# One block from the similarity sums to the rounded adjacency, rows searched in pairs, parts added by TensorE

## The reference

```python
def _ada_gcn(xn, weight, bias):                    # xn: N=512 nodes, B=64, L=128; weight is adj
    x_norm = xn / jnp.maximum(jnp.linalg.norm(xn, axis=-1, keepdims=True), 1e-12)
    mean_sim = jnp.einsum('nbl,mbl->nm', x_norm, x_norm) / B
    k = max(int(N * 0.3), 1)                       # 153
    _, idx = jax.lax.top_k(mean_sim, k + 1)
    ...
    A = jnp.where(mask, mean_sim, 0)               # the k largest of each row, without itself
    deg = A.sum(axis=0)
    dinv = jnp.where(deg > 0, jax.lax.rsqrt(deg), 0)
    An = dinv[:, None] * A * dinv[None, :]
    xw = jnp.einsum('nbl,lo->nbo', xn, weight)
    out = jnp.einsum('sd,sbl->dbl', An, xw) + bias
    return out
...
x = _layernorm(x + _L0_gnn_ref(x, adj, L0_gnn_bias), axis=-1)       # _ada_gcn
x = _layernorm(x + _L1_gnn_ref(x, adj, ...), axis=-1)               # two kernels over 128 nodes, W matrices
x = _layernorm(x + _L2_gnn_ref(x, adj, L2_gnn_bias), axis=-1)       # _ada_gcn
x = _layernorm(x + _L3_gnn_ref(x, adj, adj, L3_gnn_bias), axis=-1)
```

## Time and profile before

| | |
|---|---|
| median of 3 runs | 1784.02 us (1780.71 to 1786.39) |
| the profiled execution | 1781.9 us, of which the span is 1779.8 us |
| busy share PE, DVE, ACT, POOL | 88%, 72%, 47%, 31% |
| mean granted clock of PE | 0.931 of full speed |
| DMA | 106.14 MB, 59 GB/s over the span |

### The profile page before, as it was taken

One profiled execution on the slowest core, in us unless ns is written; L12 is line 12 of the kernel. 1 busy time (PEld: TensorE's weight loads), 2 busy tenths in 40 slices (PEclk: granted clock), 3 DMA queues, 4 the chain that ended last, 5 costly groups with the idle time before them and its releaser, 6 DMA issues. The chain is left out here.

```text
span 1779.8 us, 27351 instructions
## 1 busy us (share of the span) xinstructions
PE 1557.4 (88%) x7776; PEld 1268.6 (71%) x7776; DVE 1286.9 (72%) x3046; ACT 828.6 (47%) x1381; POOL 548.3 (31%) x749
## 2 busy tenths in 40 slices
PE   7899470599999999999999999998599791799997
PEld 4678330478888888888888888876488691577775
DVE  5798799347766677666776667765477699599997
ACT  7775220134344443444434444343333591377775
POOL 5652020012123221232212322122100000599997
PEclk9999685799999999999999999999699895799998
DMA  5320200101001110011100111000442000244442
GB/s 210 106 72 1 94 0 0 47 25 42 24 30 47 47 41 23 30 47 47 41 22 31 47 47 41 18 12 25 171 143 95 0 0 0 71 144 146 145 143 106
DMA packets 57580, 106.14 MB, mean 60 GB/s; under 512 B 5888, under 2 KB 6016, under 8 KB 57536
## 3 DMA queue, kind: packets, MB, share of 16 engines
q1 hardware_dynamic: 57536, 105.60, 17.7%
HBM read 71.90 MB, written 33.69 MB: 59 GB/s over the span
## 5 line engine op out<-in xcount | busy, mean ns | idle before, releaser
L773 POOL TENSOR_TENSOR rs_a<-ve_a,neghalf 128x1 f32<-128x1 f32 x64 | 34.6, 541 | 495.4 <-DVE nm_a L767 495.4
L232 PE MATMUL acc<-xn_lo,xn_hi 128*128 128x512 f32 (+1 forms) x640 | 145.4, 358 | 5.0 <-DVE xn_lo L203 4.8
L198 ACT ACTIVATE xn_hi<-xn 128x512 fp32r<-128x512 f32 x128 | 80.6, 630 | 117.1 <-DVE xn L191 117.0
L232 PEld LDWEIGHTS acc<-xn_lo,xn_hi 128*128 128x128 f32 x640 | 102.3, 192 | 19.2 <-DVE xn_lo L203 10.4
L1566 PE MATMUL l_ps<-an_hi,xw_hi 128*128 128x512 f32 x256 | 105.5, 412 | 9.8 <-POOL xw_lo L1627 8.4
L223 PEld LDWEIGHTS acc<-xn_hi 128*128 128x128 f32 x512 | 95.6, 192 | 24.3 <-ACT xn_hi L198 7.7
L923 PE MATMUL l_ps<-an_hi,xw_hi 128*128 128x512 f32 x256 | 103.2, 403 | 6.5 <-DVE xw_lo L1263 6.3
L564 DVE MATCH_REPLACE8 work<-best,work 128x520 f32<-128x520 f32 x160 | 107.7, 685 | 0.0
L329 POOL TENSOR_TENSOR sq_lo<-sq,sq_hi 128x512 fp32r<-128x512 f32 x64 | 87.3, 1380 | 61.2 <-ACT sq_hi L296 61.0
L203 DVE TENSOR_TENSOR xn_lo<-xn,xn_hi 128x512 fp32r<-128x512 f32 x128 | 105.8, 827 | 0.4 <-ACT xn_hi L198 0.2
L923 PE MATMUL l_ps<-an_hi,xw_lo 128*128 128x512 f32 x256 | 101.3, 396 | 0.0
(11 more groups left out here) (239 smaller groups left out, 4869.5 us busy)
## 6 DMA issues: line engine op xcount, KB each, us to landing
xr<-in_x SPq DMA_DIRECT2D x32, 512.0 KB, 3.5
xin<-in_x SPq DMA_DIRECT2D x64, 256.0 KB, 2.6
between<-xo SPq DMA_DIRECT2D x64, 256.0 KB, 2.0
xres<-between SPq DMA_DIRECT2D x32, 512.0 KB, 3.7
xin<-between SPq DMA_DIRECT2D x64, 256.0 KB, 2.7
out<-xo SPq DMA_DIRECT2D x64, 256.0 KB, 2.0
raw_lang<-in_L_gnn_W_lang SPq DMA_DIRECT2D x1, 1024.0 KB, 5.5
raw_grav<-in_L_gnn_W_grav SPq DMA_DIRECT2D x1, 1024.0 KB, 7.9
```

The lines of the kernel that those rows point to most:

```text
L198: self.nc.scalar.activation(self.hi[:, i % 4, :], self.xn[:, i % 4, :], ACT.Copy).then_inc(self.hi_ready, 1)
L232: mm = self.nc.tensor.matmul(out, h[:, c * P:(c + 1) * P], l[:, a:b], start=False, stop=False, skip_group_check=True)
```

## The change

The three functions `whole_similarity`, `choose` and `normal_adjacency` become one function `adjacency` with one block; the two barriers between them are gone, and semaphores take their place. In particular:

- `hl` is copied to SBUF by ACT (rows 0 and 1) and DVE (rows 3 and 2) without the factor 1/64, which is now applied at the degrees.
- Row 0 of the similarity is put together as before (transposes into a bank, two additions on DVE). For the rows 1, 3 and 2 PE adds the transposed blocks of `hl_sb` and `hl_sb` itself right into the banks of `hh`, with products with the identity; ACT copies the finished rows to SBUF. The blocks under the diagonal are transposed into three different banks.
- The search takes two rows at a time: all 20 rounds of the rows 0 and 1, then all of the rows 2 and 3. It begins when rows 0 and 1 stand in `work`. Marked entries are kept (now in `sim` itself) after each pair. The masks of rows 2 and 3 come between the pairs.
- PE sums the degrees of rows 0 and 1 between the pairs. ACT takes the square root and DVE the reciprocal, in place of GpSimd's power; ACT computes a root of a small tile beforehand.
- GpSimd takes the remainders of the rows 0 and 1, DVE those of 2 and 3.
- All eight PSUM banks are held through similarity and adjacency; `an_hi` and `an_lo` and the tiles for the weights are allocated before the similarity. The weights' loads are issued at the start of the block.

```diff
+            def largest(p):
+                pair = (2 * p, 2 * p + 1)
+                dve.sem_inc(marked[p], 2)
+                with dve.Fori(0, rounds) as r:
+                    for k, c in enumerate(pair):
+                        dve.wait_ge(marked[p], 2 * r + k + 1)
+                        own_step(dve, passed)
+                        nc.vector.max(best[:, c, :], work[:, c, :]).then_inc(found[p], 1)
+                    for k, c in enumerate(pair):
+                        dve.wait_ge(found[p], 2 * r + k + 1)
+                        own_step(dve, passed)
+                        mark(p, c)
...
+                dve.wait_ge(lower, CH - 1)
+                for k, c in enumerate(pair):
+                    dve.wait_ge(marked[p], 2 * (rounds + (1 if rest else 0)) + k + 1)
+                    nc.vector.scalar_tensor_tensor(out=sim[:, c, :], in0=row_of(c), scalar=CHOSEN, in1=sim[:, c, :],
+                                                   op0=ALU.is_equal, op1=ALU.mult).then_inc(chosen, 1)
+
+            nc.vector.tensor_copy(hl_sb[:, 3, :], at.hl[3]).then_inc(dve_hl, 1)
+            nc.vector.tensor_copy(hl_sb[:, 2, :], at.hl[2]).then_inc(dve_hl, 1)
+            nc.vector.memset(work[:, :, 0:8], NEVER)
+            dve.wait_ge(act_hl, 1)
+            nc.vector.tensor_tensor(part, at.hh[0], hl_sb[:, 0, :], ALU.add).then_inc(parted, 1)
+            dve.wait_ge(t0_made, 1)
+            dve.wait_ge(parted, 1)
+            nc.vector.tensor_tensor(sim[:, 0, :], g[:], part, ALU.add).then_inc(row0, 1)
...
+            dve.wait_ge(copied, 1)
+            mask(1)
+            dve.wait_ge(masked, 2)
+            largest(0)
+            dve.wait_ge(copied, 3)
+            mask(2)
+            mask(3)
+            dve.wait_ge(masked, 4)
+            largest(1)
+
+            dve.wait_ge(summed, 1)
+            nc.vector.tensor_scalar(deg[:], g[:, 0:CH], 1.0 / nb, 1e-37, ALU.mult, ALU.max).then_inc(dve_done, 1)
+            nc.vector.tensor_scalar(pos[:], g[:, 0:CH], 0.0, None, ALU.is_gt).then_inc(dve_done, 1)
+            dve.wait_ge(rooted, 1)
+            nc.vector.reciprocal(root[:], root[:]).then_inc(dve_done, 1)
...
+            for c in (2, 3):
+                dve.wait_ge(hi_ready, c + 1)
+                nc.vector.tensor_tensor(s.an_lo[:, c, :], row_of(c), s.an_hi[:, c, :].bitcast(F32), ALU.subtract)
...
+            def add_turned(out, c, j):
+                nc.tensor.matmul(out, hl_sb[:, j, c * P:(c + 1) * P], s.ident[:], start=False, stop=False,
+                                 skip_group_check=True)
+
+            def add_plain(out, row):
+                return nc.tensor.matmul(out, s.ident[:], row, start=False, stop=True, skip_group_check=True)
...
+            for j in range(1, CH):
+                add_turned(at.hh[1][:, (j - 1) * P:j * P], 1, j)
+            add_plain(at.hh[1][:, 0:P], hl_sb[:, 1, P:2 * P])
+            add_turned(at.hh[3], 3, 3)
+            add_plain(at.hh[3], hl_sb[:, 3, 3 * P:N]).then_inc(raised, 1)
+            for j in range(2, CH):
+                add_turned(at.hh[2][:, (j - 2) * P:(j - 1) * P], 2, j)
+            add_plain(at.hh[2], hl_sb[:, 2, 2 * P:N]).then_inc(raised, 1)
+            for c in range(1, CH):
+                pe.wait_ge(row0, 1)
+                if c > 1:
+                    pe.wait_ge(upper, c - 1)
+                for j in range(c):
+                    mm = nc.tensor.transpose(turned[c][0][:, j * P:(j + 1) * P], sim[:, j, c * P:(c + 1) * P], s.ident[:])
+                mm.then_inc(low_made, 1)
...
+            act.wait_ge(raised, 1)
+            copy(sim[:, 1, P:N], at.hh[1]).then_inc(upper, 1)
+            act.wait_ge(low_made, 1)
+            copy(sim[:, 1, 0:P], h[:, 0:P]).then_inc(lower, 1)
+            act.wait_ge(lower, 1)
+            act.wait_ge(upper, 1)
+            copy(row_of(1), sim[:, 1, :]).then_inc(copied, 1)
...
+            act.wait_ge(warmed, 1)
+            nc.scalar.activation(warm[:], warm[:], ACT.Sqrt)
+            act.wait_ge(dve_done, 2)
+            nc.scalar.activation(root[:], deg[:], ACT.Sqrt).then_inc(rooted, 1)
```

More of the change, by code:

```diff
@@ L754, in first @@
+            for c in (0, 1):
+                pool.wait_ge(hi_ready, c + 1)
+                nc.gpsimd.tensor_tensor(s.an_lo[:, c, :], row_of(c), s.an_hi[:, c, :].bitcast(F32), ALU.subtract)
 def first(g):
```

404 lines of the change are left out of this document (176 added, 228 removed).

## The result

The changed kernel takes 1764.88 us (median of 4 runs, 1761.68 to 1768.1) against 1783.01 (4 runs, 1780.71 to 1786.39): ratio 0.9897, 95% interval 0.9872 to 0.9922. In a second series it was 1763.89 against 1784.28, ratio 0.9876 (0.9855 to 0.9897). The forecast was 1768, range 1760 to 1777. The profiled execution took 1764.64 us, its span is 1762.8.

The account below looks back on a forecast made before the run. DVE's serial chain, with the PE-DVE-ACT chain around it, was taken to bound both adjacencies. Terms 10.0 + 3.8 + 2.3 - 0.15 = 16.0 us off; from the runs' median of 1784.0, forecast 1768 us, range 1760 to 1777.

Parts of the forecast that it names:

- Ahead of the search: From the similarity's products to the first MAX8: 5.3 and 4.65 us off in the two adjacencies, 10.0 together.
- the unit of PE's products: One 128x128 fp32 product ahead of the search, two instructions: 0.265 us at full clock, 0.52 at half; ten units.
- The moment of the fall that I assumed: PE's clock halves ahead of the search, 2.9 and 2.2 us after ACT's first copy in the two adjacencies.
- The two PSUM copies: DVE's two copies of 512 columns out of PSUM, ahead of the search: 1.3 us for both.
- Search, choice and sums: From first MAX8 to summed degrees: 108.6 us instead of 110.48, 1.9 off in each adjacency, 3.8 in all.
- 0.76 for a block end: Price of a block end in DVE's chain at the search: 0.76 us, one of them gone.
- Behind the sums: From summed degrees to last difference: 0.65 + 0.5, 1.15 us off in each adjacency, 2.3 in all.
- the split of the differences: Behind the sums, GpSimd and DVE each take two differences: 0.5 us off in each adjacency.
- The table: The exponential's table is loaded again in the second turn of the pair of layers: 0.15 us lost.
- The loop of two rows: Rival: search turns with two rows stall; small gap, 1772 to 1783 us, chance 0.12; slower than before, 0.07.
- Time given back behind: Rival: stages behind the adjacency give the gain back, leaving under 5 us; no chance of its own, within 0.12.
- layers that change by more than 2 us: Sign that the prediction is wrong: the layers' stretch, whose code is unchanged, changes its length by over 2 us.

Follow-up runs that it names:

- e2: The changed kernel with its four rows searched in one loop again instead of in pairs; 1774.79 us, ratio 0.994.
- e3: The changed kernel with its two inner block ends back, before and after the search; pairs and PE's additions kept; 1776.82 us, ratio 0.9951.
- e8: The changed kernel with nine products of constants on PE between the similarity's last product and the first transpose; 1763.78 us.
- e11: The changed kernel with the row order of e7, five products of constants in the head, and the added products of e9 and e10; 1755.40 us, ratio 0.9842.
- e12: e11 with eleven instead of five products behind the last round, three instead of five behind the sums, eight instead of ten at the next stage's start; 1755.23 us.
- e10: e9 with further products of constants: 5 between sums and row of degrees, 22 behind it, 10 at the next stage's start; 1762.51 us, ratio 0.988.
- e7: The changed kernel with PE's transposes of row 1's lower block moved ahead of row 2's additions; 1765.08 us, ratio 0.9885.
- e9: The changed kernel with five products of constants on PE behind each of the second pair's last five rounds, before the sums; 1760.19 us.

## Why the prediction was right, point by point

- *Ahead of the search*: 10.0 us forecast, 14.2 in the first profile, 12.7 with the clock fallen in both (8.55 and 8.61). The term that was mis-sized is the unit of PE's products, at both clocks: I took 0.265 and 0.52 us, the length of a group of four units divided by four, which counts the tail of the group's last instruction in every unit. From start to start a unit is 0.42 us at half clock (1388.77, 1389.19), and from the first addition to row 1's turned block it is 3.85 us in the second head, not 5.1; at full clock it is 2.22 in the first head (191.14 to 193.36), where ten units of 0.265 make 2.65. A further 0.3 us came off behind PE. The moment of the fall that I assumed is no property of the place: the clock fell or stayed in the first heads of executions of one program. (Of the eight additions on DVE that, by the section on the change, have left it, two are still there, L562 and L565; six have gone.) The two PSUM copies (1.3) and the start of PE (1.35 forecast, 1.46) were right.
- *Search, choice and sums*: 3.8 forecast, 3.8 measured, and the steps between (51.1 us for pair 0, row 2 chosen at 104.3) stand where they were put. e2 and e3 show that pairs and missing block ends bring it. In the price of the parts 0.76 for a block end was too much by e3's 0.3, as above.
- *Behind the sums*: 2.3 forecast, 1.3 measured. The root brought its 0.65 each; the split of the differences, put at 0.5, brought nothing. I had DVE's pair at 0.98 a piece from the earlier trace rows; beside GpSimd it was 1.2, and DVE is only free for it (310.6) when it could as well begin four.
- *The table*: 0.15 forecast, nothing measured, since ACT waits 2.40 us behind it.
- *The loop of two rows*: no stall. *Time given back behind*: none shown to be the change's. One of the prediction's own signs of being wrong, layers that change by more than 2 us, did come, with 3.8 us; but two executions of the kernel before differ by 4.2 us there as well, so the sign was set tighter than the program repeats. The 3.8 us belong to the clock's moments, and they explain why 19.2 us of the stretches showed as 17.0 of the span.
- With the clock fallen in both heads, 12.7 + 3.8 + 1.3 = 17.8 us; the medians differ by 18.1 and 20.4. The forecast of 16.0 was short by 2.7 us in the heads and long by 1.0 in the ends; that these two errors go against each other is luck: with the ends right and the heads as forecast the sum is 15.1.

## What to carry to other kernels

A block end between stages cost 0.3 us of waiting in e3 and 0.8 in the kernel before; what the two ends forbid, that the next stage starts on the first half of its data, cost another 4.4 us an adjacency in e3, and it is found by asking what the first waiting instruction really needs. Where a serial stretch holds PE's small products, price them at both clocks, from one start to the next and not from a group's length. If PE has idle time right ahead, products of constants that end just before the real ones may begin kept the clock in six heads of six (e8, e11, e12); what that is worth in the whole time is less sure, since e10 gained nothing that can be told and e12 no more than e11. Compare stretches of the trace, and profile one program twice, before a difference of 4 us in 1000 is put down to an edit.

## What the runs showed of the chip

- One program's unchanged stretch of layers takes 1064.0 or 1067.8 us, the other's 1064.0 or 1068.2, by where the granted clock is at half.
- The clock fell behind gaps of 2.0 and about 0.9 us in PE's work (before the sums and before the row of degrees), and held behind 2.3 us in four first heads of nine (changed kernel, e7, e9, e10): the length of a gap alone does not decide.
- An fp32 product of 128x128 starts 0.22 us after another at full clock and 0.42 to 0.43 at half.
- A difference of 128x512 takes DVE 0.62 us of a row of four alone, and 1.19 beside the same operation on GpSimd, which takes 1.25: two engines together do four no sooner than DVE does.
- GpSimd's power of 128x4 took 1.03 us, ACT's root of it 0.20 and DVE's reciprocal 0.18.
